# Loading the even A22 weights ahead of the filter stores in one DMA queue of a LoRA plus state-space kernel

## What is computed

```python
# layer 0: a dense product with a low-rank adapter per sequence
A, Bw = lora_A_w[adapter_ids], lora_B_w[adapter_ids]          # rank 16, 32 adapters
x = x + (x @ base_weight.T + base_bias + (x @ A.T) @ Bw.T)    # per sequence, 1024 x 1024
# layer 1: a causal convolution over the 1024 columns, per head
P = dtA[:, :, None] * jnp.arange(1024)
K = 2.0 * jnp.einsum('hn,hnl->hl', Ct, jnp.exp(P)).real       # filter of each head, 64 complex states
y = irfft(rfft(x, 2048) * rfft(K, 2048))[..., :1024] + x * D[:, None]
x = x + y * (jnp.arange(1024) < length)
```

## Time and profile before

| What | Value |
|---|---|
| median of 3 runs | 1060.03 us (1059.44 to 1060.83) |
| the profiled execution: its own time | 1061.48 us |
| the profiled execution: its span, first to last instruction | 1059.8 us |
| mean granted TensorE clock | 0.998 |
| PE busy | 1050.7 us, 99% |
| DVE busy | 853.8 us, 81% |
| ACT busy | 717.4 us, 68% |
| queue of SP (q1) | 283.26 MB, 80.4% of 16 DMA engines |

### The profile page before, as it was taken

How to read it: one execution, slowest core, us unless ns; L and a number is a source line. 1 busy time by engine, 2 the same in 40 slices (tenths; PEclk the granted TensorE clock), 3 DMA queues, 4 the chain that set the end, 5 groups by cost and what they waited for, 6 DMA issues and landing times.

```text
span 1059.8 us, 21414 instructions
## 1 busy us (share of the span) xinstructions
PE 1050.7 (99%) x7992; PEld 1020.7 (96%) x7992; DVE 853.8 (81%) x1287; ACT 717.4 (68%) x1260; POOL 28.3 (3%) x79
## 2 busy tenths in 40 slices
PE   9999999999999999999999999999999999999998
PEld 7999999999999999999999999999999999999997
DVE  7899887878798887878678787877488888888887
ACT  5756546755748566566557567465598888889885
POOL 0000000000000000000000000000000000000000
PEclk9999999999999999999999999999999999999999
DMA  8577769698977989878886889778798978888873
GB/s 301 193 249 278 238 224 293 192 313 254 291 229 250 255 258 298 249 261 239 259 262 216 282 255 288 237 265 254 269 364 297 337 299 330 314 314 337 285 276 139
DMA packets 164747, 284.63 MB, mean 269 GB/s; under 512 B 10979, under 2 KB 125860, under 8 KB 149284
## 3 DMA queue, kind: packets, MB, share of 16 engines
q1 hardware_dynamic: 164644, 283.26, 80.4%
HBM read 193.96 MB, written 89.26 MB: 267 GB/s over the span
## 4 chain that ended last, share of the span: by engine, by line
PE 90%; DVE 4%; DMA 2%; ACT 1%; issue 1%; SPq 1%; DVEq 0%; ACTq 0%
PE acc L1856 34%; PE acc L2018 25%; PE acc L1862 17%; PE acc L1784 5%; PE acc L1828 5%; PE acc L2053 3%; PE acc L1794 2%; DMA wq_raw<-state_scratch 1%; DMA state_scratch<-e_sb 1%; DMA x_raw<-x_t 1%; DVE x_sb L1303 0%; DVE xt_lo L1146 0%; SPq L521 0%; PE acc L1963 0%; ACT xt_hi L724 0%
## 5 line engine op out<-in xcount | busy, mean ns | idle before, releaser
L1856 PE MATMUL acc<-xt_hi,w_pair 128*128 128x256 f32 x1680 | 213.9, 279 | 1.9 <-issue 1.9
L1856 PE MATMUL acc<-xt_hi,v_hi 128*128 128x256 f32 x896 | 212.6, 278 | 0.2 <-ACT acc L724 0.2
L1856 PE MATMUL acc<-xt_hi,v_lo 128*128 128x256 f32 x896 | 212.4, 277 | 0.0
L1856 PEld LDWEIGHTS acc<-xt_hi,w_pair 128*128 128x128 f32 x1680 | 203.7, 189 | 2.1 <-issue 2.1
L1856 PEld LDWEIGHTS acc<-xt_hi,v_hi 128*128 128x128 f32 x896 | 168.4, 188 | 0.4 <-ACT acc L724 0.4
L1856 PEld LDWEIGHTS acc<-xt_hi,v_lo 128*128 128x128 f32 x896 | 168.5, 188 | 0.0
L1706 DVE COPY_PREDICATED out_sb<-mask,acc 128x1024 f32<-128x1024 uint8 (+1 forms) x65 | 85.8, 1321 | 46.6 <-PE acc L2018 46.5
L2018 PE MATMUL acc<-u_hi,f_hi 128*128 128x512 f32 (+1 forms) x320 | 123.2, 385 | 0.1
L724 ACT ACTIVATE acc<-acc 128x512 f32<-128x512 f32 x93 | 54.0, 582 | 100.0 <-PE acc L1862 94.8
L2018 PE MATMUL acc<-u_lo,f_hi 128*128 128x512 f32 (+1 forms) x320 | 117.6, 367 | 0.0
L2018 PE MATMUL acc<-u_hi,f_lo 128*128 128x512 f32 (+1 forms) x320 | 117.5, 367 | 0.0
(11 more groups left out here) (201 smaller groups left out, 2152.7 us busy)
## 6 DMA issues: line engine op xcount, KB each, us to landing
w_pair<-weight_scratch SPq DMA_DIRECT2D x71, 1024.0 KB, 5.7
x_scratch<-x_sb SPq DMA_DIRECT2D x32, 1024.0 KB, 8.5
out<-out_sb SPq DMA_DIRECT2D x63, 512.0 KB, 4.8
x_raw<-x_t SPq DMA_DIRECT2D x30, 1024.0 KB, 9.1
u_raw<-x_scratch SPq DMA_DIRECT2D x14, 2048.0 KB, 11.9
wq_raw<-state_scratch SPq DMA_DIRECT2D x16, 1024.0 KB, 8.3
a_raw<-lora_a SPq DMA_DIRECT2D x128, 64.0 KB, 3.1
b_raw<-lora_b SPq DMA_DIRECT2D x128, 64.0 KB, 2.1
```

Of the source, the lines that this page charges most:

```text
L1856: pe.matmul(by_row(bank_part(bank, i)), w[:, k, i, :], hi[:, k, :, :], start=opens and i == 0 and k == 0 and s == 0, stop=False, skip_grou ...
```

## The change

From group 2 on, `load_ws(g, A22)` stands directly behind the adapter rows A and ahead of `filter_stores(g, 0)`, and in the last group also ahead of `store_unit`, the waits for the x stores and `load_u(0)`. Group 1 keeps the old place. Nothing else is changed: no instruction is added or removed, and the load waits for the same semaphores.

```diff
                 if g == 1:
                     store_sum(S4, 0)
+                else:
+                    load_ws(g, A22)
                 filter_stores(g, 0)
                 if g == LAST:
                     store_unit(ALL_UNITS - 1)
@@
                         sp.wait_ge(st_x1[par], 16 * g)
                     sp.wait_ge(c_t["T4"], n_groups)
                     load_u(0, LAST)
-                load_ws(g, A22)
+                if g == 1:
+                    load_ws(g, A22)
                 if g < LAST:
                     load_x(g + 1, 1)
```

## The result

| What | Before | After |
|---|---|---|
| median of the timed runs, us | 1060.32 (1059.44 to 1060.83, 4 runs) | 1072.78 (1070.88 to 1082.51, 4 runs) |
| the profiled execution, us | 1061.48 | 1072.04 |
| its span, us | 1059.8 | 1070.3 |
| ratio of the times | | 1.0143, 95% interval 1.0112 to 1.0173 |

The change makes the kernel 1.4% slower, 12.5 us by the medians and 10.5 us by the two spans. 1062.3 was forecast, with a range up to 1066.4, so the time lies 6.4 us above the range. The kernel after also varies more from execution to execution: its four runs lie within 11.6 us, the four of the kernel before within 1.4 us (and the 17 to 25 that were timed of it later, set by set, within 2.9 to 4.3 us).

A forecast was written before the change was run, and what follows sets the result against it. The prediction took PE, busy in 99% of the span, to bound the kernel. Its terms, -3.6 + 1.2 + 4.7 = +2.3 us, added to the 1060.03 us median gave 1062.3 us, range 1057.0 to 1066.4.

The forecast's parts named there:

- part 2: Groups 3, 5, 6, 8, 9, 11, 13, 14: passed stores land later; PE waits 0.6 us in 9 and 14, 1.2 us together.
- part 3: Last group: filter load wq_raw lands 3.4 us late, PE waits 3.1 us and loses 1.6 at lower clock; costs 4.7 us.
- part 1: Group 10: A22's load goes out earlier, ending PE's 1.94 us wait and 1.64 us at lower clock; gain 3.6 us.
- rival D: Slower still, chance 0.22: no gain in group 10, or timed runs have less wait to lose; costs only, +5.9 us, 1065.9.
- I count 0 for these six: Groups 3, 5, 6, 8, 11 and 13: later stores cost PE nothing, 0 us.
- the same queueing delays it by about 2 us: Groups 3, 5, 8, 11, 13: DVE's unit starts about 2 us later, inside 3 us of slack.
- That is 755.9: Last group: landing time of the filter load wq_raw by the queue sum, 3.4 us late.
- B: Faster, chance 0.13: wq_raw lands in time in the last group, no cost there; about 1057.0 us.
- C: Same, chance 0.15: stores not held by the load in front; +1.1 us, 1061.1, or 1059.5 if the clock stays up.
- (1): Group 10: p4 starts without idle, its 16 matmuls take 2.0 us, A22's load lands in 5 to 6 us.
- (2): Groups 9 and 14: DVE's store waits grow from 2.0 and 2.2 to about 6.5 us each; PE shows two short waits.
- (3): Last group: ACT's wq_raw wait grows from 3.1 to about 6.5 us, PE waits about 3, clock falls to 0.5.

The follow-up runs named there:

- five_groups: Kernel before, with A22's load moved to its new place only in groups 5, 8, 9, 13 and 14: 1067.13 us, ratio 1.0086.
- store_after_landing: As five_groups, but SP holds the filter stores until A22's load has landed: 1073.70 us, ratio 1.0128 against the kernel before.
- last_wait_only: Kernel before, old order, with SP waiting for p3 ahead of the last group's e_sb stores: 1065.70 us, ratio 1.0050.
- wait_only: Kernel before, old order, with SP waiting for p3 ahead of the filter stores in groups 5, 8, 9, 13, 14: 1059.25 us, ratio 0.9995.
- only_10: Kernel before, with A22's load moved to its new place in group 10 alone: 1058.33 us, ratio 0.9990.
- after_again: The changed kernel timed once more without an edit, against the kernel before: 1079.00 us, ratio 1.0188.
- all_but_last: Kernel before, with A22's load moved to its new place in groups 2 to 14, not the last: 1066.14 us, ratio 1.0069.

## Why the prediction was wrong

The three mechanisms are the ones that the prediction named. What failed are the sizes: the cost of part 2 was nearly six times too small and that of part 3 a third too small, and the gain of part 1 was one execution's.

**Part 1, "Gain 3.6 us".** In the profiled executions it is right to 0.1 us: the wait and the half clock went, 3.7 us. As a term for the median it was too large: alone it is worth 1.1 us. The step that failed is "I carry the difference over to the median" while the whole wait stayed in the sum. The profiled execution lay 1.4 us above the median, and rival D had named the reason: the others had less of that wait to lose.

**Part 2, "1.2 us together" and "I count 0 for these six".** Here the largest error lies. It came to 6.9 us in the profiled execution and 7.9 in the timed runs. Three steps failed:
- "lands 4.7 us later". That is the lowest value of the earlier trace rows, from loads without a store right behind them. With one it is 5.8 to 6.5 us, as `five_groups` beside `store_after_landing` shows, and up to 7.8 in other executions. The 1 us more was in the bounds, but not in the sum.
- "the same queueing delays it by about 2 us". The e_sb stores of group 8 land at 418.7, where they had landed at 413.5. The estimate covers only one half of that: the second store goes out 2.1 us later (412.26 for 410.15), since A22 and the end of the adapter rows come first, and it lands 6.4 us after its issue in place of 3.4, behind A22's megabyte. A delay of 5 us doesn't fit 3 us of slack.
- "So PE waits 0.6 us in each". With both groups at 7.6 us of DVE wait instead of 6.5, it was 1.5 us in each.

The forecast was right on who waits for whom, also that the short waits leave the clock up in this execution, but took this for the rule: in other executions waits of 1.84 us and more lost it.

**Part 3, "costs 4.7 us".** Mechanism right, and the clock's 1.6 us right to 0.2 (7.4 us less PE's wait of 6.0). The term that was too small is the landing of the filters, "That is 755.9": 16.4 us after A22's issue, where it was 19.4. Counted from A22's issue, A22 was 1.2 us later than summed (5.9 for 4.7), u_raw 2.0 (landing 13.5 us on, for 11.5) and the filters 3.1: so 1.2 us for A22, 0.8 for the stores and u_raw, and 1.1 for the filters. The sentence "SP's own wait is no hole in the queue" was right, and confirmed by `last_wait_only`, where filters issued 4.6 us sooner landed hardly sooner. Nor was the rate of "390 GB/s that this stretch ran at" too high. The window from A22's landing to that of the filters, after:

```profile
748.58:762.12 13.54, 9.93 (x85) 9.73 (x84) 3.11 (x10) 1.81 (x3) 0.00 (x0) 0.96 1.04 406
```

At 406 GB/s 5.5 MB moved in these 13.5 us, where the sum has 4.13 MB. What it left out is the second u_raw load: SP issues it right behind the filters, at 752.18, and the two move side by side for 9.9 us. Before, it went out at 747.98, 4.5 us ahead of the filters' landing, so that the same sum came out right there to 0.6 us. In `last_wait_only` it stands beside the filters for 9.9 us too. How much of the delay is its own was not tried: no run holds it back.

**The rivals.** B (the filters in time) didn't happen. C, by which the stores would not be held by the load in front, is refuted: in `wait_only`, without that load in front, the waits of part 2 are gone. The Trainium skill's page "DMA: Bandwidth & Descriptors", section "Queues, rings and completion order", was quoted by half. It also says that a semaphore's increment lands only after every earlier write of that engine. By that a store on the same DMA engines can't report ahead of the load in front, whatever its data do, and the trace agrees: in group 9 it lands 1.4 us behind the load. D was nearest, at +5.9: its gain of 0 is closer to the 1.1 us than the forecast's 3.6, but its costs are the forecast's own and fell short the same way.

**What would show it.** Of the three signs that the prediction named, (1) was seen in group 10, but for A22's landing (6.8 us, not 5 to 6). Of (2) the two waits of DVE came at 7.6 us for 6.5, but PE had four waits and not two, and longer ones. Of (3) ACT's wait was 9.5 us for 6.5 and PE's 6.0 for 3.

**What stays open.** The changed kernel costs 12.5 us in the first runs and 19.7 in the later ones, the parts add up to 14.0, and the costs of groups 8 to 14 make 6.9 or 11.9 of it. The two profiled executions show the difference in longer waits in groups 8 and 14 and in one more stretch of lower clock. These waits follow the store's landing, and the landing follows SP's adapter rows and A22's own time; why the rows take 5.9 us in one execution and 4.0 in another, and A22 6.1 or 7.7 us in the same group, is open. The parts and the later runs of the whole change also ran on different chips, and whether that plays a part was not tried.

## What to carry to other kernels

A store that stands behind a load in the same queue lands behind it: here 7 us after its issue with 1 MB in front, in place of 3. The load itself goes slower for having the store behind it. So before such a move, list every engine that rewrites the stored buffers and its slack, in all groups, also in those in which nobody waits yet. If one transfer is what makes a load late, move that one (zb, 1.1 us won here), not the load past everything. And a term read from one execution's wait should be compared with how far that execution lies from the median.

## What the runs showed of the hardware

- A 1 MB load with a 0.5 MB store issued 0.4 us behind it on the same queue took 5.8 to 6.5 us, and 4.6 to 5.0 us with the store held back (`five_groups`, `store_after_landing`). The store landed 1.4 us behind the load, 7.1 us after its issue, and 3.2 us after it without the load in front (group 9, kernels after and before).
- TensorE's granted clock fell to its lower level (1.2 GHz) behind waits of 1.84, 1.94, 1.95, 2.06, 2.17, 2.60 and 3.38 us (and the longer ones of the last group), and stayed at 2.4 GHz behind others of 1.86, 2.00, 2.13 and 3.12 us, and behind all up to 1.7. So waits of 1.84 us and more went either way here. In layer 0's groups 8 to 14, where the clock fell, the group lost 1.6 to 1.8 us beyond the wait; where it stayed up, 0.3.
- With the exponent load zb, 0.5 MB, and 0.5 MB of stores in front, A22 landed 9.0 to 10.5 us after its issue (eight executions); with the stores alone in front 6.4 and 7.7 us; with neither in front, but both behind it, 5.8 to 7.3 us (`only_10`, after, `after_again`, `all_but_last`).
